# A perceiver block: the row product and the inversion moved inside two of sixteen quads

## The reference

```python
q = (x @ Wq + bq).reshape(B, N, NUM_HEADS, HEAD_DIM)
k = (y @ Wk + bk).reshape(B, M, NUM_HEADS, HEAD_DIM)
v = (y @ Wv + bv).reshape(B, M, NUM_HEADS, HEAD_DIM)
scale = 1.0 / np.sqrt(HEAD_DIM)
scores = jnp.einsum('bnhd,bmhd->bhnm', q, k) * scale
attn = jax.nn.softmax(scores, axis=-1)
out = jnp.einsum('bhnm,bmhd->bnhd', attn, v).reshape(B, N, IMAGE_DIM)
h = jax.nn.relu(out @ W1 + b1)
return h @ W2 + b2
```

## Time and profile before

| | |
|---|---|
| median of three runs | 1385.34 us |
| profiled execution, span | 1383.2 us |
| PE busy | 1332.2 us, 96% |
| DVE busy | 1120.9 us, 81% |
| ACT busy | 806.1 us, 58% |
| POOL busy | 778.7 us, 56% |
| attend stage | about 343 to 1116 us of the span |

### The profile page before, as it was taken

One profiled execution on the slowest core, in us unless ns is written; L12 is line 12 of the kernel. 1 busy time (PEld: TensorE's weight loads), 2 busy tenths in 40 slices (PEclk: granted clock), 3 DMA queues, 4 the chain that ended last, 5 costly groups with the idle time before them and its releaser, 6 DMA issues. The chain is left out here.

```text
span 1383.2 us, 39979 instructions
## 1 busy us (share of the span) xinstructions
PE 1332.2 (96%) x17098; PEld 702.8 (51%) x17098; DVE 1120.9 (81%) x1786; ACT 806.1 (58%) x1459; POOL 778.7 (56%) x320
## 2 busy tenths in 40 slices
PE   7999999998999999999999999999999999999898
PEld 4444444443555555555555555545555445566454
DVE  5778888887888888888888888888887746578895
ACT  4454444443777777776777776776777841354332
POOL 0322222122899988988998898899889100201121
PEclk9999999999999999999999999999999999999999
DMA  8568777786352122122212112211210030491000
GB/s 265 177 169 231 207 211 211 210 238 177 91 183 69 39 69 67 30 65 67 69 39 68 56 38 69 67 50 57 59 66 31 5 145 1 92 214 41 0 9 23
DMA packets 127799, 137.54 MB, mean 99 GB/s; under 512 B 44995, under 2 KB 108995, under 8 KB 125699
## 3 DMA queue, kind: packets, MB, share of 16 engines
q1 hardware_dynamic: 127622, 134.98, 34.6%
HBM read 75.70 MB, written 44.17 MB: 87 GB/s over the span
## 5 line engine op out<-in xcount | busy, mean ns | idle before, releaser
L1297 DVE TENSOR_REDUCE early<-attend_banks 128x1 f32<-128x512 f32 x952 | 612.4, 685 | 80.8 <-PE attend_banks L1042 75.6
L1261 ACT ACTIVATE attend_prob<-attend_banks 128x512 f32<-128x512 f32 x1024 | 536.0, 599 | 200.8 <-PE attend_banks L1079 198.6
L1439 POOL TENSOR_TENSOR early<-early,attend_prob 128x1024 f32<-128x1024 f32 x210 | 614.5, 2926 | 37.7 <-ACT attend_prob L1261 9.6
L1079 PE MATMUL attend_banks<-early,k_first 97*32 97x512 f16 x2560 | 258.9, 382 | 3.1 <-ACT attend_prob L1261 3.1
L1042 PE MATMUL attend_banks<-k_first,early 96*32 96x512 f16 x2272 | 235.1, 382 | 1.1 <-PEq L285 1.1
L1079 PE MATMUL attend_banks<-early,attend_k_rest 97*32 97x512 f16 x1536 | 154.1, 381 | 2.8 <-ACT attend_prob L1261 2.8
L1042 PE MATMUL attend_banks<-attend_k_rest,early 96*32 96x512 f16 x1536 | 155.8, 380 | 0.0
L1103 PE MATMUL attend_banks<-attend_prob,ones 128*32 128x128 f32 x3048 | 134.3, 272 | 3.6 <-DVE attend_recip L1309 3.6
L1092 PE MATMUL attend_banks<-attend_prob,wkv_area 128*32 128x512 f32 x1024 | 134.1, 592 | 0.0
L1092 PE MATMUL attend_banks<-attend_prob,attend_vh_odd 128*32 128x512 f32 x1024 | 133.6, 592 | 0.0
L503 POOL TENSOR_TENSOR project_w_whole<-project_grid,project_qscale 128x704 f32<-128x704 f32 x24 | 33.3, 1386 | 173.0 <-DVE project_grid L636 173.0
(11 more groups left out here) (220 smaller groups left out, 1823.6 us busy)
## 6 DMA issues: line engine op xcount, KB each, us to landing
v_scratch<-project_v SPq DMA_DIRECT2D x16, 1024.0 KB, 8.9
early<-in_ctx_dram SPq DMA_DIRECT2D x16, 768.0 KB, 6.2
k_first<-k_scratch SPq DMA_DIRECT2D x36, 256.0 KB, 3.5
k_scratch<-project_k_hi SPq DMA_DIRECT2D x64, 128.0 KB, 2.9
k_scratch<-project_k_lo SPq DMA_DIRECT2D x64, 128.0 KB, 3.1
attend_vh_odd<-v_scratch SPq DMA_DIRECT2D x8, 1024.0 KB, 5.0
wkv_area<-v_scratch SPq DMA_DIRECT2D x7, 1024.0 KB, 4.8
attend_k_rest<-k_scratch SPq DMA_DIRECT2D x24, 256.0 KB, 3.5
```

Of the source, the lines that this page charges most:

```text
L1079: last = nc.tensor.matmul(s_ps[c * HD:(c + 1) * HD, s_bank[n], :], key_rows[:, c * HD:(c + 1) * HD], q_stack[0:KROWS + 1, h, :], start=Tru ...
L1261: nc.scalar.activation(prob[:, q % PSLOTS, t, :], s_ps[:, s_bank[BT * q + t]], ACT.Exp, scale=SCALE).then_inc(p_ready, 1)
L1297: nc.vector.tensor_reduce(part_max[:, s, j, part:part + 1], pre_ps[:, bank], AX.X, ALU.max).then_inc(pre_read, 1)
L1439: nc.gpsimd.tensor_tensor(sums, sums, prob[:, q % PSLOTS, 0:n], ALU.add).then_inc(pool_summed, 1)
```

## The change

The row of the next head is made inside quad 14, between the second score product and the denominators, and not behind its weighted values. ACT's copy moves with it, to behind the second exponential of quad 14, and the row's turn in the ring of maximum banks moves from behind the four products of quad 14 to between the second and the third. In quad 2 the denominators go behind the four score and four maximum products, and DVE inverts behind the quad's first two maxima (in the last head, which has no maxima, at the start of the quad as before).

```diff
 PE_ORDER = ((0,), 0, (1,), 1, "den", 2, (2,), 3, (3,))
+PE_ORDER_INVERT = ((0,), 0, (1,), 1, 2, (2,), 3, (3,), "den")
+PE_ORDER_ROW = ((0,), 0, (1,), 1, "row", "den", 2, (2,), 3, (3,))
...
-            OUTPUT_AT, ROW_AT = 5, QUADS - 2
+            OUTPUT_AT, ROW_AT, INVERT_AT = 5, QUADS - 2, 2
             turns_of_head = []
             for q in range(QUADS):
-                turns_of_head += [(q, j) for j in range(TT)]
-                turns_of_head += ["output"] if q == OUTPUT_AT else ["row"] if q == ROW_AT else []
+                tiles = [(q, j) for j in range(TT)]
+                turns_of_head += tiles[:2] + ["row"] + tiles[2:] if q == ROW_AT else tiles
+                turns_of_head += ["output"] if q == OUTPUT_AT else []
...
                         ahead = last >= (1 if q < QUADS - AHEAD else 2)
-                        for step in PE_ORDER:
-                            if step == "den":
+                        order = PE_ORDER_INVERT if q == INVERT_AT else PE_ORDER_ROW if q == ROW_AT else PE_ORDER
+                        for step in order:
+                            if step == "row":
+                                if last >= 1:
+                                    n = turn_of["row"]
+                                    pe.wait_ge(pre_read, tiles_read(h, n - PRE_BANKS))
+                                    row(h + 1, 1 - s, n % PRE_BANKS)
+                            elif step == "den":
...
-                        if q == ROW_AT and last >= 1:
-                            n = turn_of["row"]
-                            pe.wait_ge(pre_read, tiles_read(h, n - PRE_BANKS))
-                            row(h + 1, 1 - s, n % PRE_BANKS)
...
                             nc.scalar.activation(prob[:, q % PSLOTS, t, :], s_ps[:, s_bank[BT * q + t]], ACT.Exp,
                                                  scale=SCALE).then_inc(p_ready, 1)
+                            if q == ROW_AT and t == 1 and last >= 1:
+                                copy_row(h + 1, turn_of["row"] % PRE_BANKS)
                         if q == 0 and not first:
                             read_pv(*before)
-                        if q == ROW_AT and last >= 1:
-                            copy_row(h + 1, turn_of["row"] % PRE_BANKS)
...
-                        if q == 2 and not first:
+                        inverting = q == INVERT_AT and not first
+                        if inverting and last == 0:
                             invert(*before)
...
                                 tile_max(s_of, part, j, TILES * h + TT * q + j,
                                          turn_of[(q, j)] % PRE_BANKS)
+                                if inverting and j == 1:
+                                    invert(*before)
```

## The result

| | before | after |
|---|---|---|
| median | 1386.04 us (4 runs) | 1393.57 us (4 runs, 1392.61 to 1394.56) |
| span of the profiled execution | 1383.2 us | 1390.8 us |

The ratio is 1.0054, 95% interval 1.0038 to 1.007: slower by 7.5 us, where 1392.4 us and +7.1 were forecast.

The account below looks back on a forecast made before the run. PE was taken as the bound, busy 544.85 of 550 us in the attend stage. Quad 2 +8.7, row and copy -1.3, head 15 -0.4, head 0 +0.1 gave +7.1 us: 1392.4 us, range 1388 to 1399.

Parts of the forecast that it names:

- The wait and its cause, quad 2: Quad 2, heads 1 to 14: inversion 1.50 us later, PE's need 0.87 later; wait grows from 0.39 to about 1.0 us.
- two maxima take half of 2.61, 1.30 us: Quad 2 on DVE: the inversion begins 1.30 us after the first maximum begins, half of four maxima's 2.61.
- Row and copy: Quads 14 and 15: the copy no longer delays quad 15's first exponential; -0.09 us a head, -1.3 us in 14 heads.
- the lag passes through every later group: From quad 14 on: the row holds one column group 0.22 us, delaying later groups until PE waits, wherever the row stands.
- about 0.66 in head 15: Quad 2 of head 15: the changed profile would show a wait of about 0.66 us on the denominators, released by DVE's inversion.
- the forecast's own -0.4 there: Quad 2 of head 15: two score products go ahead of the denominators into a 0.66 us wait; -0.4 us, between -0.66 and 0.
- The +0.1 us of head 0: Quad 2 of head 0, which inverts nothing: later denominators and perhaps a waiting fourth score product; +0.06, summed as +0.1 us.
- The sum: Whole kernel: +8.7 - 1.3 - 0.4 + 0.1 = +7.1 us, put on the median as 1392.4 us, 0.5% slower.
- The clock: Rival, chance 0.04: PE's clock falls at quad 2's new wait in each of 14 heads; 24 us more, 1416 us.
- The row leaving the chain: Rival, chance 0.09: the row's 0.22 us is hidden in quad 14; a head gains 0.31, total +4.1, 1389.4 us.
- The inversion in time: Rival, chance 0.04: quad 2's inversion ends before the denominators are due, the 0.39 us wait goes; -7.1, 1378.2 us.
- Row or copy late: Rival, chance 0.06: PE waits for the head maximum or delayed exponentials, up to 0.59 us a head; 1402 us.

Follow-up runs that it names:

- the row part alone: The kernel before with only the row, its ring turn and its copy moved, quad 2 put back: ratio 0.9993 [0.9983, 1.0003] to the kernel before.
- the run with idle times of 1.60 us: The kernel before with quad 2's inversion behind two maxima and the denominators left between the second and third score product: ratio 1.0143 to the kernel before.

## Why the prediction was right

**The wait and its cause, quad 2: right in mechanism, a little too dear.** The forecast was 3.85 us for quad 2 and +0.62 us for it in each head; it is 3.76 and +0.52. Of the steps, the first maximum 0.45 us after the product (594.62 to 595.07), the inversion's 0.95 us and PE's follow-up of 0.05 us held. The term "two maxima take half of 2.61, 1.30 us" did not: the inversion begins 1.20 us after the first maximum (595.07 to 596.27), before the second one's recorded end. The same overlap was to be read in the earlier trace rows, where the maxima begin at 593.81 and the inversion ends at 593.89. Counting by starts and not by lengths gives 0.09 us less a head, 1.3 us in 14 heads.

The wait was said to be about 1.0 us (595.45 less 594.43) and is 0.81: 0.12 less because the inversion was through earlier, 0.10 of it by the two maxima, and 0.09 less because PE came later: its fourth score product waited for its exponential (596.02, 1.40 us after the quad's start, for 1.37 said). That this wait is covered by the longer one behind it held.

**Row and copy: right in sign and size.** Quads 14 and 15 together 6.49 us for 6.46 said, a head 0.06 to 0.07 us less for 0.09. The row did not leave the chain: the row part alone gained the copy's delay and no more. That the lag passes through every later group was right only up to one row's time.

**The rest.** Head 15 gained 0.31 us for the 0.4 said. The sign "about 0.66 in head 15" did not come, and it did not fit the forecast's own -0.4 there: the inversion (1085.19 + 0.94 = 1086.13) is through ahead of the denominators at 1086.32, and PE waits for an exponential instead:

```profile
1086.09 0.40 PE L1082 MATMUL attend_banks<-early,k_first 97*32 97x512 f16 x4 [0.34 <-ACT attend_prob L1266]
1086.32 0.61 PE L1106 MATMUL attend_banks<-attend_prob,ones 128*32 128x128 f32 x16
```

The +0.1 us of head 0 doesn't show: from the first product of the stage to the inversion of head 1 the changed kernel takes 1.63 - 0.28 = 1.35 us more, and the inversion's later place and the row part alone give 1.41 - 0.06. No new wait came in quad 3. For the head maximum the row waited only once, in head 14 as said; its weight loads there, in a timeline:

```profile
1074.51 0.11 PEld L1069 LDWEIGHTS attend_banks<-identh,early 128*1 128x1 f16 x2 [0.46 <-DVE early L1302]
```

The maximum ran from 1074.17 to 1074.39, the matmuls began at 1074.54, where without it they would have come at 1073.92 + 2 x 0.22 = 1074.36: 0.18 us late, for 0.2 said.

**The sum.** The attend stage is 5.8 us longer in the profile, for 7.1 said; the measured parts add up to 14 x (0.52 - 0.06) - 0.3 = 6.1. The medians differ by 7.5, with an interval of 5.3 to 9.7 us that holds both. That 1393.57 comes so close to 1392.4 is therefore in part luck: the profile supports about 6 us, and the scatter behind the stage, 1.5 us from one execution to the next, is about as large as what is left over.

**Rivals.** The clock: out by the run with idle times of 1.60 us. The row leaving the chain: out by the row alone. The inversion in time: not so in the changed kernel, but it came true once the denominators stood behind the weighted values, where quad 2 fell by 0.32 us against the kernel before, for the 0.39 at which this rival was priced. Row or copy late: out, as quads 14 and 15 are no longer than before.

## What to carry to other kernels

When a producer and the consumer that waits for it are both moved back in their queues, compute both new times from the same start. While the wait stays, the change is worth the difference of the two shifts; where it goes, it is worth at most the old wait, and less if another wait stands behind it (0.12 of 0.39 us with the inversion first and the denominators last). Here +1.41 us on DVE against about 0.9 on PE lost 0.5%, and one place further on PE won 0.4%. The row's small matmuls stayed on the way of a full PE in both places; moving them took away only the 0.06 us that the exponential had queued behind the copy of the row. A difference of some us in a kernel of 1.4 ms is better read from the heads in the profile than from the total.

## What was not expected of the hardware

- Matmuls of the next group began in three column groups while the row's were still being issued in the fourth (582.53 against 582.59), so the row hardly delays the others at first (quad 14 is 3.13 us where it was 3.06); with eight row matmuls in place of four they began 0.22 us later.
- A DVE instruction of another kind can begin 0.08 to 0.09 us ahead of the recorded end of the one before it (596.27 against 595.07 + 1.29 = 596.36; 597.14 against 596.27 + 0.95 = 597.22).
- PE idle times of up to 1.60 us inside the attend stage left the clock at 1.00, while at the start of the feed-forward layer an idle time of 1.50 us was followed by 0.67 in one execution and by 1.00 in another of the same program.
